# Runs of constant products in the tensor engine's waits of a two-layer graph transformer with routed experts

## What is computed

```python
xn = _layernorm(x)
x = x + gat(xn, src, dst) + linear_attention(xn)        # layer 0
x = x + moe_768x768(_layernorm(x))                      # 8 experts, top 2
xn = _layernorm(x)
x = x + gcn2(xn, edge_index) + hydra_attention(xn)      # layer 1: two 768x768 convolutions
x = x + moe_384(_layernorm(x))                          # 8 experts, top 2, gelu between two matmuls
```

## Time and profile before

| | us |
|---|---|
| median of 3 runs | 2000.32 |
| range of these runs | 1999.68 to 2001.61 |
| the profiled execution | 1999.16 |
| its span, first to last instruction | 1997.3 |
| TensorE busy (matmuls) | 1838.2, 92% of the span |
| VectorE busy | 745.1, 37% |
| ScalarE busy | 401.4, 20% |
| GpSimd busy | 128.5, 6% |
| mean granted TensorE clock | 0.964 of 2.4 GHz |

### The profile page before, as it was taken

The page is one execution under the profiler, slowest core; times in us unless marked ns, Lnnn a source line. Parts: engine busy times, 40 slices in busy tenths (PEclk is TensorE's granted clock), DMA queues, the critical chain, the costliest instruction groups (busy, mean ns, idle before and its releaser), DMA issues.

```text
span 1997.3 us, 24539 instructions
## 1 busy us (share of the span) xinstructions
PE 1838.2 (92%) x8418; PEld 1157.3 (58%) x8419; DVE 745.1 (37%) x1688; ACT 401.4 (20%) x1065; POOL 128.5 (6%) x212
## 2 busy tenths in 40 slices
PE   7999999999899999599997999999999999599980
PEld 4555566567533344366666955555588589366550
DVE  3212222597789989411115311151111123311114
ACT  2431210024312212101102421000221211221210
POOL 0000000000000000111114000000000000111105
PEclk9999999999999999699998999999999999699995
DMA  6004000000000101545556111010010011544537
GB/s 185 0 1 150 19 0 1 21 1 1 21 31 31 49 24 42 205 141 189 189 182 180 46 48 48 0 48 0 1 48 1 0 56 47 205 141 174 189 115 235
DMA packets 58060, 153.06 MB, mean 77 GB/s; under 512 B 12526, under 2 KB 23170, under 8 KB 57525
## 3 DMA queue, kind: packets, MB, share of 16 engines
q1 hardware_dynamic: 34053, 87.05, 12.7%
q0 software_dynamic: 13120, 35.86, 6.0%
q10 hardware_dynamic: 10800, 28.98, 4.0%
HBM read 121.37 MB, written 33.99 MB: 78 GB/s over the span
## 4 chain that ended last, share of the span: by engine, by line
PE 81%; DVE 8%; DMA 5%; issue 2%; DVEq 2%; ACT 1%; POOL 1%; ACTq 0%; SPq 0%; POOLq 0%
PE PS L646 23%; PE PS L975 10%; PE PS L656 8%; PE PS L795 5%; PE PS L1016 4%; PE PS L1085 4%; PE PS L717 4%; PE PS L1105 4%; PE PS L1057 4%; DVE WRA L1730 4%; PE PS L1043 3%; PE PS L884 2%; DMA WS<-in_fW 2%; PE PS L893 2%; DVE WRB L1730 2%
## 5 line engine op out<-in xcount | busy, mean ns | idle before, releaser
L646 PE MATMUL PS<-WS,XT 128*125 128x384 f32 x960 | 313.0, 488 | 1.4 <-issue 1.4
L646 PEld LDWEIGHTS PS<-WS,XT 128*125 128x125 f32 x960 | 180.1, 189 | 129.4 <-issue 3.3
L975 PE MATMUL PS<-WS,XGT 128*128 x600 | 199.7, 490 | 0.0
L975 PEld LDWEIGHTS PS<-WS,XGT 128*128 128x128 f32 x600 | 113.2, 192 | 74.6 <-issue 2.2
L656 PE MATMUL PS<-XT,WS 128*128 128x416 f32 (+1 forms) x432 | 151.2, 512 | 0.0
L1730 DVE SCALAR_TENSOR_TENSOR WRA<-RB,U,AT 125x500 f32<-125x500 f32 (+1 forms) x240 | 140.1, 648 | 8.5 <-ACT AT L1205 6.6
L1859 DVE TENSOR_TENSOR YS<-PS,EBB 128x768 f32<-128x768 f32 x48 | 46.0, 958 | 255.3 <-PE PS L975 191.8
L656 PEld LDWEIGHTS PS<-XT,WS 128*128 128x128 f32 x432 | 81.6, 189 | 69.2 <-issue 69.2
L884 PE MATMUL PS<-WRA,F 125*64 125x500 f32 (+1 forms) x480 | 100.1, 535 | 10.1 <-DVE WRA L1730 9.5
L1085 PE MATMUL PS<-WS,XGT 128*128 x288 | 99.6, 497 | 7.7 <-DMA WS<-in_fW 4.9
L1105 PE MATMUL PS<-WS,HT 128*128 x276 | 92.9, 486 | 2.5 <-ACT HT L1417 2.5
(11 more groups left out here) (293 smaller groups left out, 2229.7 us busy)
## 6 DMA issues: line engine op xcount, KB each, us to landing
WS<-in_ewT SPq DMA_DIRECT2D x8, 2304.0 KB, 10.7
expert_rows<-YS ACTq DMA_DIRECT2D x48, 384.0 KB, 2.3
WS<-in_fW SPq DMA_DIRECT2D x16, 1152.0 KB, 7.7
WS<-in_w SPq DMA_DIRECT2D x5, 2304.0 KB, 10.4
xn_rows<-XN ACTq DMA_DIRECT2D x20, 336.0 KB
RB<-expert_rows SPq DMA_DIRECT2D x12, 488.3 KB
WS<-in_wp SPq DMA_DIRECT2D x2, 2304.0 KB, 11.9
WS<-in_W SPq DMA_DIRECT2D x2, 2304.0 KB, 8.1
```

The source lines that it names most:

```text
L646: last = nc.tensor.matmul(ps[0:T, 0:HC], lhsT[:, k, t * T:(t + 1) * T], w[:, k, b * HC:(b + 1) * HC], start=(k == 0), stop=(k == KC - 1))
L975: last = nc.tensor.matmul(PS[:, 4 + 2 * a + b, 0:HC], XGT[:, a, k, :], WS[:, bass.ds(slot, 1), k * C + b * HC:k * C + (b + 1) * HC].rearra ...
```

## The change

A new function `awake(m, n)` issues n matmuls of constants: `onesb` as weights, `before` repeated three times as 375 columns (bf16), into the bank of job m, with nobody waiting for the result and no semaphore. It is called at ten places of TensorE's code, four of which are in `route`, which runs for both layers. At the start 24 matmuls of `ident` with `ident` (fp32, 128 columns) go into a bank that the first keys will use. Where the bank may still hold something, `begin` is called first. The wait for the last logits (`lg_emptied`) moves into `route`, behind the first run there.

```diff
+        def awake(m, n):
+            for _ in range(n):
+                nc.tensor.matmul(bank(m)[0:T, 0:3 * T], onesb, before.unsqueeze(1).to_broadcast([T, 3, T]), start=True, stop=True)
+
         pe.wait_ge(consts, 1)
+        for _ in range(24):
+            nc.tensor.matmul(bank(J.at["kv0"])[:, 0:P], ident, ident, start=True, stop=True)
...
         projected(NT - 1)
+        m = J.at[f"proj0_{NT - 1}"] + 2
+        begin(m)
+        awake(m, 14)
         pe.wait_ge(table_ready, 1)
...
         pe.wait_ge(f_ready, 1)
+        awake(3, 6)
...
         turned_unit(len(UNITS) - 1)
+        awake(3, 14)
         for t in range(LATE, NT):
...
             logits1(t)
-        pe.wait_ge(lg_emptied, NT)

         def route(L):
             k = 1 if L == 1 else 2
+            if L == 1:
+                free = 3
+                awake(free, 13)
+                pe.wait_ge(lg_emptied, NT)
+            else:
+                free = J.at[f"tokens{L}"] + 1
+                begin(free)
+                awake(free, 13)
             pe.wait_ge(sel_ready, k)
...
             nc.tensor.matmul(ps[0:T, n:n + NE], onesb, SUMS[:, :, NT - 1], start=True, stop=True).then_inc(pe_filled, 1)
+            awake(free, 14)
             ps = begin(J.at[f"tokens{L}"])
...
             last.then_inc(pe_filled, 1)
+            awake(free, 14)
             m = J.at[f"tokens{L}"]
...
         last.then_inc(pe_filled, 1)
+        awake(J.at["lnt2_1"], 28)
         for t in (0, 1):
             transpose_tile(2, t, J.at[f"lnt2_{t}"])
...
             rows(J.at["conv2"] + 2 * t, XT, w, t)
+        begin(J.at["agg2_0"])
+        awake(J.at["agg2_0"], 6)
         pe.wait_ge(hf_used, 40)
...
+            if t == NT:
+                begin(J.at[f"lnt3_{t - 2}"])
+                awake(J.at[f"lnt3_{t - 2}"], 4)
             if 2 <= t < NT + 2:
                 transpose_tile(3, t - 2, J.at[f"lnt3_{t - 2}"])
```

## The result

| | before | after |
|---|---|---|
| median, 20 runs each | 2000.05 us (1995.38 to 2003.24) | 1994.97 us (1989.13 to 1998.49) |
| ratio, 95% interval | 1 | 0.9973 (0.9966 to 0.9979) |
| the profiled execution, its span | 1999.16, 1997.3 us | 1994.83, 1993.0 us |
| mean granted clock | 0.964 | 0.975 |

5.1 us less, where 6.8 was forecast. Single executions of either kernel spread over 8 to 9 us, more than the change moves, so the sum is judged by the medians, and each place by stages of the profiles, of which there are fourteen (before, after and twelve experiments). "After" is the changed kernel.

A forecast was written before the change was run, and what follows sets the result against it. TensorE's half-clock stretches were the most to win, only where TensorE is waited for. Terms 0.5 + 0.4 + 0.3 + 1.4 + 1.6 + 0.8 + 1.2 = 6.2 us gave 1993.0, stated as 1993.5; range 1986.5 to 1999.

The forecast's parts named there:

- the cost of nothing: All added runs go ahead of waits: long ones fit even at half clock, short ones at full clock; cost 0.
- The rival in which runs outlast their gaps: Products taking over 0.37 us overrun the waits of the two routings; 2018 us at 0.6 us each; chance 0.05.
- L775 and the turn to layer 1, both 0: VectorE sets the pace at L775, gathered rows at the turn to layer 1; gain 0 at both.
- L1057, 1.6: Wait before L1057, TensorE on the path: 6 products leave 0.9 of 1.86 us idle; gain 1.6 us.
- L884, 0.4: Before L884, 6 products: slow TensorE shows only in VectorE's wait for L831; gain 0.4 us, from 0 to 0.4.
- First routing, 0.3: First routing ahead of the gather: about 1.6 us in all, but 3.2 us stay idle; taken 0.3 us.
- First experts, 1.4 of 3.1: First experts, 14 products behind L932: faster second transposes and first 24 products; taken 1.4 us of 0 to 3.1.
- Second routing, 0.8 of 2.2: Second routing ahead of the gather, from transposes to last logit: 2.2 us to be had, 3.4 at most; taken 0.8.
- Second experts, 1.2: Second experts: 0.7 us for transposes plus 12 L1085 in 3.87 instead of 6.04, 2.9 together; taken 1.2 us.
- The start, 0.5: 24 fp32 products at the start against the cold first 48 L646; bounds 0 and 1.6 us, taken 0.5.
- The rule on transposes: Transposes don't count as busy for the clock gate: start worth 0, not 0.5; kept open within the 0.28 fall-again rival.
- The sum: Seven places add to 6.2 us off the profiled 1999.16; forecast 1993.5, 6.8 us under the median.

The follow-up runs named there:

- long_double: Changed kernel with the seven long runs of the routings doubled and the 4 ahead of the last transposes made 8; 1995.58 us, 0.9982 of the kernel before.
- the extended kernels: Three kernels from the changed one, runs resized and placed only where they can pay, one with the start run put back; 0.9964, 0.9953, 0.9946 of before.
- no_zero_places: Changed kernel without the 24 products at the start, the 14 before L775 and the 28 at the turn to layer 1; 1994.72 us, 0.9978 of before.
- short_only: Changed kernel with only the 6 products before L884 and the 6 before L1057 left; 1997.13 us, 0.9989 of the kernel before.
- routes_only: Changed kernel with only the runs of the two routings and the 4 ahead of the last transposes; 1994.81 us, 0.9979 of the kernel before.
- extended_2: Changed kernel without start, L775 and layer-turn runs, with new short runs and most others resized, third set; 1989.65 us, 0.9953 of before.
- start_wide: Changed kernel with 8 products of 384 columns at the start in place of 24 of 128; 1999.29 us, 1.0010 of the kernel before.
- no_start: Changed kernel without the 24 products at the start, nothing else; 1995.93 us, 0.9992 of the kernel before.
- changed_2: The changed kernel as it was, measured again in the third set; 1992.68 us, 0.9963 of the kernel before.

## Why the prediction was right, point by point

**What bounds the kernel, and the cost of nothing.** Right. Added products took 2.27 us for 13 at full clock and 4.63 for 14 at half (estimates 2.1 and 4.5), and in the changed kernel none was still running when its wait ended. The rival in which runs outlast their gaps came true in long_double, where 28 took 6.34 us, and in small in the extended kernels (18 in 5.83).

**L775 and the turn to layer 1, both 0.** Right, shown by no_zero_places and by the stages. That rested on looking for who sets the pace behind the half-clock stretch: VectorE's one-hots and the gathered rows behind XN.

**L1057, 1.6.** Measured 1.57 (97.53 to 95.96 in short_only). The reading that 1.86 us idle is dangerous and 0.9 isn't was right. But the term was taken as if before always fell there; routes_only didn't, so over many executions it is worth less than 1.6.

**L884, 0.4.** Measured 0.7 in after. But with that run the stage takes 278.94 (extended_2) to 281.86 us (start_wide), and without it 281.20 (routes_only) and 281.32 (before). It varies by more than the term, so neither 0.4 nor 0 is shown.

**First routing, 0.3.** Mis-sized by its odds: the price of 1.6 was right (1.5 measured), but 3.2 us of idle time let the clock fall in 3 of 7 profiles, not nearly always. The step that failed is from "more than what let the clock fall elsewhere" to "Taken 0.3"; 0.9 would have been the mean, 1.5 in 4 of 7.

**First experts, 1.4 of 3.1.** L924 to L998 changed by 1.0 us in after (0.3 lost ahead of the experts, 1.3 won in them). Over the seven profiles with 14 behind L932, L975 to L998 is 210.6 to 212.7 us, a mean of 1.2 below before. With five products between the transposes it is 210.6 each time, 2.1 below.

**Second routing, 0.8 of 2.2.** The largest miss: 2.60 us. The step that failed is the sum of its cold work: it was capped at 2.2 and then cut to 0.8 because "the work behind is thin". Through the thin work (transposes, logits and ScalarE's copies) the clock held, in six of the seven kernels that had 4 products there; in no_start it fell, and L1057 to the second L924 took 95.09 us instead of 93.4.

**Second experts, 1.2.** The transposes and the start came (L924 to L1085 is 1.04 us shorter), the first twelve L1113 too (4.15 against 6.04), but 1.7 of it went back one group later (5.82 against 4.13), and L1085 to end is 1.92 us more than before. What the prediction left out is the wait of 2.45 us ahead of the last L1105: it has no run, and the clock fell there in after (1.70 us) and not in before. That is luck of the two profiled executions, since it fell in half of all profiles. In the eleven profiles besides before, after and changed_2 the stage lies between 265.6 and 268.3 us, and in changed_2 it is 269.95, a spread larger than the whole term.

**The start, 0.5.** By the profile wrong: the first 48 L646 gained nothing (17.36 us; over fourteen profiles the same with and without the run), and adding 96 instructions made a stop of 1.2 us in L706's stage that the prediction didn't look for. By the times of two pairs it was no loss, though the overlapping intervals would allow one. Why the two disagree is open.

**The rule on transposes.** The Trainium skill ("TensorE: Matmul & The Clock Gate", Part 4) had it that transposes don't count as busy for the gate as matmuls do. By that rule the start would be worth 0, which is what the profile shows, though the waits around the transposes explain it as well. The experiment with 33 transposes, in which the clock rose from 0.52 to 0.98, goes against the rule as stated. The measurement decides: they count. Whether they count for less than matmuls is not shown.

**The sum.** The profiled execution is 4.3 us below that of before and the median 5.1 below, where 6.2 and 6.8 were forecast. That is the balance of misses both ways: 1.2 and 1.8 too little at the routings, and too much at the start (0.5 taken, 1.7 lost in the profile) and in the last stage. The range was wide enough; the central value owes something to luck.

## What to carry to other kernels

Ask at each place who is waited for: of the nine places of the prediction four or five were worth anything. Size a run to what it must leave, not to what it adds. Here 0.9 to 1 us idle ahead of dense products held in all 17 cases, 1.9 us in 10 of 24; between sets of transposes even 1 us wasn't safe. A run that may start at half clock must still fit at twice its length. Look for long waits to the very end of the path, as the one ahead of the last L1105. And added instructions can move a stop in TensorE's stream, so look again at the densest stage after adding any.

## What was not expected

- A stop of 1.05 to 1.2 us at a fixed place of the instruction stream, in the stage where instructions are densest (480 in 7.2 us), and later by 32 records of that stage when 64 instructions are taken from the start.
- Transposes alone lift the clock: 19 records in 3.4 us at 0.52, then 0.98.
- The same idle time, 3.19 and 3.20 us, had the clock fall in one kernel and stay in the other, and so did 1.87 and 1.86 us at L1057 and 2.45 us at the last L1105. Nothing that the profiles show of the kernels at these places tells which of the two happens.
- start_wide, 3.4 us slower in the median than no_start in the same set, for an edit in the first 10 us. Nothing in its profile explains it.
